# A step in another order on every engine: windowed top-k attention with adaptive layer norm on one core

## The reference

```
mod = silu(c) @ wmod                      # shifts, scales, gates of both halves
h   = layernorm(x) * (1 + ca) + sa
q   = relu(h @ enc_q);  v = relu(h @ enc_v)       # 8 heads of 16
m   = softplus(base + 0.1 * mlp(mean of q over tokens))
per head and token t, over the 64 tokens up to t:
    dist = sqrt(sum_e m_e (q_e(t') - q_e(t))^2 + 1e-8)
    keep the 32 smallest;  w = exp(-dist), normalised
    context = sum w v(t') + gate * 0.1 * (q / |q|) @ (U V)
    o = q * context
x   = x + ga * (o @ decoder)
h   = layernorm(x) * (1 + cb) + sb
x   = x + gb * (h + sum_e gate_e * ((h @ A_e^T) @ B_e^T))     # 2 of 8 experts per batch
```

## Time and profile before

| | |
|---|---|
| median of 3 runs | 915.0 us (914.45 to 927.3) |
| span of the profiled execution | 940.7 us |
| TensorE busy / weight loads | 838.5 us (89%) / 672.4 us (71%) |
| VectorE busy | 802.6 us (85%) |
| ScalarE busy | 627.9 us (67%) |
| GpSimd busy | 465.8 us (50%) |
| mean granted TensorE clock | 0.832 of full |
| DMA | 26.95 MB, mean 29 GB/s |

### The profile page before, as it was taken

One profiled execution on the slowest core, in us unless ns is written; L12 is line 12 of the kernel. 1 busy time (PEld: TensorE's weight loads), 2 busy tenths in 40 slices (PEclk: granted clock), 3 DMA queues, 4 the chain that ended last, 5 costly groups with the idle time before them and its releaser, 6 DMA issues.

```text
span 940.7 us, 25723 instructions
## 1 busy us (share of the span) xinstructions
PE 838.5 (89%) x4437; PEld 672.4 (71%) x4437; DVE 802.6 (85%) x6746; ACT 627.9 (67%) x1862; POOL 465.8 (50%) x871
## 2 busy tenths in 40 slices
PE   5978899999999999999979799999999897988865
PEld 3446678777877778777868677787778676767654
DVE  6956998879899887878989898879788898989990
ACT  4962467666677666666768686666666786767763
POOL 2124355545556555545555564555455564646542
PEclk9977877777789777777989997777777999999965
DMA  5300000000000000000000000000000000000000
GB/s 169 91 8 24 14 22 20 25 28 21 24 25 27 27 25 20 24 26 21 24 25 27 28 27 26 26 21 24 25 19 27 25 27 26 28 26 28 26 9 9
DMA packets 49225, 26.95 MB, mean 29 GB/s; under 512 B 5512, under 2 KB 48592, under 8 KB 49104
## 3 DMA queue, kind: packets, MB, share of 16 engines
q1 hardware_dynamic: 49104, 25.90, 9.3%
HBM read 10.28 MB, written 4.19 MB: 15 GB/s over the span
## 4 chain that ended last, share of the span: by engine, by line
DVE 36%; PE 34%; issue 16%; ACT 6%; POOL 4%; DMA 2%; DVEq 0%; POOLq 0%; ACTq 0%; SPq 0%
DVE work L946 19%; DVE m L936 12%; PE psD L1114 10%; PE psC L1159 6%; PE psW L1175 4%; PE psD L1111 3%; PE psW L1186 3%; PE psW L1177 2%; ACT key L649 2%; ACT big L661 2%; PE psX L1166 2%; DMA big<-in_x 1%; PE psX L1167 1%; DVE key L758 1%; POOL big L478 1%
## 5 line engine op out<-in xcount | busy, mean ns | idle before, releaser
L946 DVE MATCH_REPLACE8 work<-m,work 128x64 f32<-128x64 f32 x1536 | 300.9, 205 | 0.0
L1114 PE MATMUL psD<-sst,tst 128*128 128x224 f32 x1024 | 270.5, 392 | 0.0
L1114 PEld LDWEIGHTS psD<-sst,tst 128*128 128x128 f32 x1024 | 225.5, 221 | 25.9 <-issue 8.5
L936 DVE MAX8 m<-work 128x8 f32<-128x64 f32 x1536 | 210.8, 208 | 0.0
L478 POOL TENSOR_TENSOR big<-work,con 128x512 f32<-128x512 f32 x128 | 162.5, 1290 | 47.7 <-ACT work L624 47.7
L457 POOL TENSOR_TENSOR hsc<-gat,rnn 128x8 f32<-128x8 f32 x64 | 13.0, 204 | 271.2 <-ACT rnn L706 271.2
L1159 PE MATMUL psC<-vst,big 128*128 128x34 f32 x1024 | 132.7, 287 | 13.7 <-ACT big L661 11.6
L1159 PEld LDWEIGHTS psC<-vst,big 128*128 128x128 f32 x1024 | 126.6, 201 | 24.6 <-issue 22.3
L946 DVE MATCH_VALUE_LOAD work<-m,work 128x8 f32 x1536 | 115.8, 75 | 0.0
L1111 PE MATMUL psD<-mask_bf,ident_bf 128*128 128x448 bf16 x256 | 106.3, 415 | 3.5 <-DVE key L962 3.5
L946 DVE MATCH_REPLACE8 work<-m,key 128x64 f32<-128x64 f32 x512 | 100.4, 205 | 0.0
(11 more groups left out here) (199 smaller groups left out, 1506.6 us busy)
## 6 DMA issues: line engine op xcount, KB each, us to landing
hst<-hT_all SPq DMA_DIRECT2D x64, 96.0 KB
tst<-qT_all SPq DMA_DIRECT2D x256, 17.0 KB
big<-in_x SPq DMA_DIRECT2D x16, 256.0 KB, 2.7
tst<-nst SPq DMA_DIRECT2D x256, 1.0 KB
xs<-in_x SPq DMA_DIRECT2D x64, 64.0 KB, 1.8
out<-yo SPq DMA_DIRECT2D x64, 64.0 KB, 1.6
sst<-nst SPq DMA_DIRECT2D x128, 3.0 KB
con<-in_consts SPq DMA_DIRECT2D x1, 549.5 KB, 5.6
```

The costliest lines, as they stand in the source:

```text
L936: last = v.max(m8[:, h], src[:, h * WIN:(h + 1) * WIN])
L946: last = v.match_replace(work[:, s, cols], m8[:, h], src[:, cols], GONE)
L1114: last = mm(bank_of(r)[:, g, 0:SW], tst[:, s, r, g], sst[:, s, g], start=False, stop=(g == NG - 1), skip_group_check=True)
```

## The change

Work is moved inside `step` on all five engines; no arithmetic, tile or semaphore is new. The fold and `bn_stats` go between the MAX8 and the MATCH_REPLACE8 of the third round, `bn_aggr` and `den` behind that round. `osp` of chunk k is transposed in TensorE's step k+2, no longer at the end of step k+1. The matmuls of the distances are those of before, on 128 rows.

```diff
 # SyncE, step
+                k = i + 1
+                if there(i, 1):
+                    need(sync, att_ready, k - 3)
+                    sync.dma_start(xs[:, (ph + 1) % 4], xc[:, bass.ds(k, 1)].squeeze(1)).then_inc(xs_in[(ph + 1) % 4], 16)
                 k = i - 3
...
 # GpSimd, step
+                k, s = i - 1, (ph - 1) % 2
+                if there(i, -1):
+                    need(pool, wt_ready, 8 * (k - 1))
+                    for w in range(2):
+                        pool.wait_ge(wsel_ready, 2 * k + 1 + w)
...
+                k, s = i - 2, ph % 2
+                if there(i, -2):
+                    pool.wait_ge(rden_ready, k + 1)
+                    pool.wait_ge(mix_step, 5 * k + 2)
...
+                    nc.gpsimd.tensor_tensor(osp[:, s], t1[:], t2[:], ALU.add).then_inc(osp_ready, 1)
...
-                k, s, s4 = i - 2, ph % 2, (ph - 2) % 4
-                if there(i, -2):
+                k, s, s4 = i - 1, (ph - 1) % 2, (ph - 1) % 4
+                if there(i, -1):
                     pool.wait_ge(rnn_ready, k + 1)
                     nc.gpsimd.tensor_tensor(hsc[:], gat[:, s4], rnn[:, s], ALU.mult).then_inc(mix_step, 1)
                     pool.wait_ge(cst_ready, 2 * (k + 1))
                     nc.gpsimd.tensor_tensor(t1[:].rearrange(h3, h=NH), cst[:, s, :, 0:HD], q, ALU.mult).then_inc(mix_step, 1)
...
                 k, s = i + 3, (ph + 3) % 2
                 if there(i, 3):
+                    wait_alone(pool, dist_ready, k - 1)
+                    nc.gpsimd.tensor_tensor(sst[:, s, :, 0:3 * WIN], qT_all[:, :, bass.ds(column(k), 3 * WIN)],
...
+                    win = qT_all[:, :, bass.ds(column(k), 3 * WIN)]
                     wait_alone(pool, pn_ready, k - 1)
                     nc.gpsimd.tensor_tensor(sqs[:, s], win, win, ALU.mult).then_inc(opnd_ready, 1)
...
 # VectorE, step
                 if there(i, 0):
-                    rounds(i, ph, 2)
+                    rounds(i, ph, 2, next_keys)
...
+                def next_keys():
+                    k, s = i + 1, (ph + 1) % 2
+                    if there(i, 1):
+                        dve.wait_ge(qhs_ready, k + 1)
...
+                    if there(i, -2):
+                        dve.wait_ge(x2_ready, i - 1)
+                        v.bn_stats(st_c[:], x2[:, ph % 2]).then_inc(stc_ready, 1)
...
 # TensorE, step
-                    need(pe, x2_ready, min(k + 2, NCH) if isinstance(k, int) else k + 2)
                     nc.tensor.transpose(pN2, n_c[:, s], ident).then_inc(pn2_ready, 1)
...
+                contexts(0)
+
+                k, s = i - 2, ph % 2
+                if there(i, -2):
+                    pe.wait_ge(osp_ready, k + 1)
+                    need(pe, yo_ready, k)
+                    nc.tensor.transpose(pO, osp[:, s], ident).then_inc(po_ready, 1)
+
+                contexts(1)
...
                 k, s = i + 2, (ph + 2) % 2
                 if there(i, 2):
+                    pe.wait_ge(s_ready, k + 1)
                     need(pe, d2_ready, k)
-                    for r in range(NR - 1):
-                        distances(s, r)
+                    for r in range(NR):
+                        last = distances(s, r)
+                    last.then_inc(dist_ready, 1)
```

More of the change, by code:

```diff
@@ L488, in step @@
+                if there(i, 3):
+                    win = qT_all[:, :, bass.ds(column(k), 3 * WIN)]
                     wait_alone(pool, pn_ready, k - 1)
                     nc.gpsimd.tensor_tensor(sqs[:, s], win, win, ALU.mult).then_inc(opnd_ready, 1)
[L490 to L494, removed]
@@ L662, in to_wts @@
                                              ACT.Copy).then_inc(wts_ready, 1)
[L664 to L670, removed]
+                weights(0)
+                weights(1)
                 k, s = i - 3, (ph - 3) % 2
@@ L714, in step @@
                     nc.scalar.activation(nst[:, s], pN, ACT.Copy).then_inc(nst_ready, 1)
+                k, s = i - 2, ph % 2
+                if there(i, -2):
+                    act.wait_ge(nb_done, k + 1)
+                    need(act, pn2_ready, k - 1)
+                    nc.scalar.activation(n_c[:, s], x2[:, s], ACT.Identity, bias=nb_c[:], scale=rs_c[:, s:s + 1]).then_inc(nc_ready, 1)
                 k, s4 = i + 2, (ph + 2) % 4
@@ L941, in rounds @@
                     wait_alone(dve, picked, 16 * i + 4 * rnd + 1 + half)
-                    if late and half == 1:
-                        late()
                     for h in range(4 * half, 4 * half + 4):
@@ new lines, in step @@
+                if there(i, 0):
+                    rounds(i, ph, 2, next_keys)
+                else:
+                    next_keys()
+                if there(i, -2):
+                    wait_alone(dve, stc_ready, i - 1)
+                    wait_alone(dve, nc_ready, i - 3)
+                    v.bn_aggr(mv_c[:, ph % 2], st_c[:]).then_inc(mvc_ready, 1)
+                k, s = i - 1, (ph - 1) % 2
+                if there(i, -1):
+                    dve.wait_ge(cst_ready, 2 * (k + 1))
+                    need(dve, rden_ready, k - 1)
+                    v.tensor_scalar(den[:, s], cst[:, s, :, HD], 1e-8, None, ALU.add).then_inc(den_done, 1)
@@ L986, in step @@
                 if there(i, 0):
[L987 removed]
+                    rounds(i, ph, 3, reciprocals)
                 else:
[L989 to L990 removed]
+                    reciprocals()
             steps(dve, step, routing)
@@ L1131, in weights_T, with contexts @@
                                                 ident).then_inc(wt_ready, 1)
-                weights_T(0)
-                s, x4 = ph % 2, (ph - 2) % 4
-                if there(i, -2):
-                    k = i - 2
-                    pe.wait_ge(xs_in[x4], 16 * (k // 4) + 16)
-                    pe.wait_ge(oT_ready, k + 1)
-                    mm(pAtt, ident, xs[:, x4], start=True, stop=False)
-                    mm(pAtt, oT[:, s], dec_b[:, bass.ds(k // CPB, 1)].squeeze(1), start=False, stop=True).then_inc(att_ready, 1)
-                weights_T(1)
+                def contexts(half):
+                    k, s, s4 = i - 1, (ph - 1) % 2, (ph - 1) % 4
+                    if there(i, -1):
+                        if half == 0:
+                            if isinstance(i, int) and i == 1:
+                                pe.wait_ge(gb_ready, 2)
+                            need(pe, cst_ready, 2 * k)
+                            pe.wait_ge(vst_ready, k + 1)
+                        pe.wait_ge(wts_ready, 2 * k + 1 + half)
+                        for h in range(4 * half, 4 * half + 4):
+                            last = mm(pC[:, h * 2 * VD:(h + 1) * 2 * VD], wts[:, s, h],
+                                      vst[:, s4, h].rearrange("p v e -> p (v e)"), start=True, stop=True)
+                        if half == 1:
+                            last.then_inc(c_ready, 1)
                 k, s = i - 3, (ph - 3) % 2
@@ L1146, in step @@
                     pe.wait_ge(nc_ready, k + 1)
[L1147 removed]
                     nc.tensor.transpose(pN2, n_c[:, s], ident).then_inc(pn2_ready, 1)
[L1150 to L1161 removed]
+                weights_T(0)
                 k, s = i - 3, (ph - 3) % 2
```

213 lines of the change are left out of this document (92 added, 121 removed).

## The result

The median went from 916.7 us (914.45 to 927.3, four runs) to **1248.97 us** (1240.64 to 1249.35, four runs): ratio 1.356, 95% interval 1.346 to 1.367. The forecast of 1185 us has the sign and the mechanism; the time is 64 us above it and 6 us under the upper end of the range of 1040 to 1255. The profiled execution took 1249.19 us with a span of 1247.4.

A forecast was written before the change was run, and what follows sets the result against it. Bound before: VectorE's 11.5 us a step, plus waits on TensorE late at half clock. After: a closed ring, 14.25 us, 16.9 with the clock; 63 steps instead of 12.91 add 251 us, end 2: 1194, taken 1185, range 1040 to 1255.

The forecast's parts named there:

- mixing's wait: GpSimd's first mixing product of chunk i-1 waits for `cst`, TensorE's contexts of the same step; `sst` and `sqs` now follow.
- The path: Distances, Relu copies, `qh`, weight copies, contexts, `cst`, mixing, `sst` and `sqs`, norms, next distances: no step can be shorter.
- the signs: Expected in the profile after: alike steps 16 to 17.5 us apart, named waits, TensorE idle about 3 us ahead of norms.
- The ring's length: Durations from one step's last distance matmul round to the next step's, all at full clock: 14.25 us.
- The clock's share: TensorE's norms and part of its distances run at half clock behind the gap, lengthening the step from 14.25 to 16.9 us.
- the gap begins at 5.8, the clock falls at about 8.0: TensorE, us after the last distance matmul: idle from 5.8 to 9.2, clock down from about 8.0 to 14.8.
- the one stall of the earlier trace: TensorE's stop at a loop head: clock fell some 2.3 us after it and stayed down 6.7 to 6.8 us.
- the offset of the profiled execution: Profiled execution of the kernel before was 25.7 us above its median: 1194 us if not constant, 1168 if constant; taken 1185.
- Ring at full clock: Rival: TensorE's gap too short, or placed so that the clock holds; 1000 to 1027 us, chance 0.13.
- Faster: Rival: GpSimd reaches `sqs` before TensorE needs it, VectorE's fold never waits; 865 to 890 us, chance 0.06.
- no difference: Rival: overlaps not counted bring the round of waits to about 12.9 us at full clock; chance 0.03.
- More than the forecast: Rival: half clock also covers contexts and `pAtt`, lengthening TensorE's gap; 17.8 to 21.5 us a step, 1250 to 1480, chance 0.14.

The follow-up runs named there:

- 1: Changed kernel with GpSimd's `sst` and `sqs` back ahead of the mixing, all other moves kept: 902.45 us, 0.960 of the kernel before.
- 2: Kernel before with one wait added, GpSimd's `sqs`, `sst` and `selm` waiting for `cst` of chunk i-1, nothing moved: 1183.4 us against 931.7.
- 3: Changed kernel with one more unread GpSimd product a step between the mixing and `sst`: 1295.4 us, step 18.44 us.
- 4: Changed kernel with one more unread GpSimd product a step, ahead of the mixing, behind `selm`: 1246.1 us, step 17.69 us.
- 6: Changed kernel with 26 unread matmuls a step spread over TensorE's idle times: 1034.1 us, step 14.34 us, clock 1.00.
- 8: Changed kernel with VectorE's `bn_stats` and its wait for `x2` behind the MATCH_REPLACE8 of the third round again: 1245.9 us.
- 7: Changed kernel with ScalarE making `h2T` between the two copies of the transposed weights again: 1329.7 us, step 18.96 us.
- 5: Changed kernel with 12 unread matmuls a step in TensorE's gap ahead of the norms: 1157.6 us, step 16.32 us, clock 0.82.
- 9: Changed kernel with TensorE's norms of chunk i+3 behind the distances of chunk i+2: 1194.8 us, step 16.91 us.
- 12: Kernel before with 10 unread matmuls a step, 6 ahead of the contexts and 4 in their middle: 891.7 us against 931.7.

## Why the prediction was right, and what it had too small

- **The move that matters.** Of all moves the forecast named one, `sst` and `sqs` behind mixing's wait. Shown: taking it back removes the slowdown (1), adding the wait alone makes most of it (2).
- **The path.** Each named wait is in the profile: `cst` at line 496, `x2` at line 981, `qh` at the fold, `sqs` ahead of line 1212 with 3.0 us a time (185.3 / 61). That GpSimd's end of the step is on it and the place behind `selm` is not is shown by 3 and 4. Two of the signs were missed: the steps are 17.70 us apart, forecast were 16 to 17.5, and they are not all alike (17.3 to 19.2).
- **The ring's length.** 14.25 us computed, 14.34 measured (6). Piece by piece in the rows of 6: norms to the last distance 612.64 - 607.65 = 4.99, where the forecast had 5.02; from there to the contexts 3.05, where it had 2.93. In the changed kernel the first piece is 611.33 - 603.21 = 8.12 and the second 3.23: of the 3.67 us by which that step (18.08) is longer than this one (14.41), 3.13 are in the norms and distances, where the forecast had put the clock's cost.
- **What cost nothing.** The place of `bn_stats` was free, as said (8). The order on SyncE was not tested by itself; it is as changed in 1, which has no slowdown. `h2T` ahead of the Relu copies was called part of the ring; that it must stay there was not seen, and 7 shows it.
- **The clock's share, the term that was too small.** 2.65 us a step was taken, 3.36 measured. The step that failed is "the gap begins at 5.8, the clock falls at about 8.0": it carried the one stall of the earlier trace rows, where the clock fell 2.3 us after TensorE stopped, over to a gap that repeats. In the rows above the clock is at 0.50 some 0.5 us ahead of the gap in one step and 1.8 us ahead in the next, and it comes back near 610, after nearly three distance groups and not after 1.75. The half-clock stretch is 10.2 us (599.5 to 609.7) and not 6.8. Laid on the forecast's ring, from 5.4 to 15.6, it costs the norms 1.04 us and makes 4.1 us of distances do the work of 2.1: a step of 17.3 us, an estimate, of the 17.70 measured. A row of a single stall gave a price for a single stall.
- **The sum.** From 1185: 63 x 0.80 = 50 us from the step, 9 us because I went between 1194 and 1168 for the offset of the profiled execution, 3 us more outside the steps, and 1.8 us between span and time: 1249. The offset was no constant: the kernel before varies from run to run (895 to 952 us over the chips used here), and the longer its time the lower its clock; the changed one took 1240.6 to 1249.35 in four runs. All these terms were short in the same direction; that the time is still inside the range, by 6 us, is in part luck.
- **The rivals.** Ring at full clock: refuted as a time, close as a length (6: 1034 against its 1000 to 1027). Faster and no difference: refuted. "More than the forecast" began at 17.8 us a step; at 17.70 its mechanism is partly there: line 1194 takes 0.65 us at 616.40 and 0.47 at 598.70, so the half-clock stretch reaches ahead of the gap in some steps.

The Trainium skill's rule on a wait that comes back with every tile (TensorE: Matmul & The Clock Gate, Part 1 and HAM oscillation) was weighed there with the one stall of the earlier trace rows behind it. This trace agrees with it in that the clock falls in nearly every step (12 times in the 12.4 steps from 500 to 720 us, 0.71 in the mean), and filling TensorE's idle time gives 1.00. Which of a step's idle times bring the fall is open: it comes ahead of the long one, and filling that one alone (5) gave 0.82.

## What to carry to other kernels

Before an instruction is moved behind one that waits, follow what waits for the moved one until it comes back to that wait; if it does within one step, the step cannot be shorter than the sum of the durations round it, whatever each engine's load. Walk it on every engine it passes, TensorE's own queue included. Where such a ring leaves TensorE a gap in every step, price TensorE's work behind the gap at half clock and do not take the stretch's length from a single stall (here it was 10.2 us, where the single stall had 6.7), and try matmuls that nobody reads in TensorE's idle times before a new order.

## What the runs showed that I had not expected

- Matmuls that nobody reads made two kernels faster, 1249 to 1034 and 1195 to 1011 us (26 and 24 a step), and brought the kernel before from a median of 931.7 to 891.7 (10 a step), where it had come by itself in one run of seven (895.2). Twelve in the changed kernel gave only 1158, with the clock at 0.82: an incomplete filling gives an incomplete return.
- The clock's cost is not the same on every ring. The changed kernel and that of 9 have filled steps of 14.34 and 14.03 us, 0.3 apart, and unfilled ones of 17.70 and 16.91, 0.8 apart. A ring made longer still shows in the step with the clock down (3: 0.74 us for a product of 0.83). Whether the clock's changes and the step fall into a common rhythm was not tested.
- VectorE loses 28 to 33 us at the heads of 13 loop passes in every kernel. It is part of the time where VectorE is the bound (1 and 12: the step there is 14.1 to 15.0 us, the others mostly 11.2 to 11.5). In 6, where the ring is the bound at full clock, the step with the loop head is 17.0 to 17.7 us and the next one 11.2 to 12.0, together two steps of 14.4: nothing is lost.
